# Projection and attention of a transformer layer put into one stage, block by block

## What is computed

```
h    = layernorm(x) * (1 + ca) + sa               # ca, sa from a small product of c
qkv  = h @ qkv_w.T ;  q, k, v per head
raw  = q . k                                      # per head, T x T
score = alpha * tanh(raw / beta) + lam * (soft . soft) / 2 + hexc . Mh . hexc / 6
        # soft = tanh(h @ hex_w.T), hexc = tanh(h @ q6_w.T): 6 columns each
attn = softmax(causal(score)) ;  out = attn @ v
x    = x + ga * (out @ out_w.T) ;  x = x + gb * experts(layernorm(x) * (1 + cb) + sb)
```

## Time and profile before

| | us |
|---|---|
| median of 3 runs | 2112.16 (2109.01 to 2115.98) |
| the profiled execution | 2128.09 |
| its span, first to last instruction | 2126.2 |
| of it, modulation | 0 to 44.2 |
| projection | 44.2 to 242.9 |
| first loads of attention, to the first exp | 242.9 to 275.7 |
| attention, first exp to last exp | 275.7 to 1322.7 |
| output and router | 1322.7 to 1584.9 |
| experts | 1584.9 to 2126.2 |

### The profile page before, as it was taken

One profiled execution on the slowest core, in us unless ns is written; L12 is line 12 of the kernel. 1 busy time (PEld: TensorE's weight loads), 2 busy tenths in 40 slices (PEclk: granted clock), 3 DMA queues, 4 the chain that ended last, 5 costly groups with the idle time before them and its releaser, 6 DMA issues. The chain is left out here.

```text
span 2126.2 us, 37447 instructions
## 1 busy us (share of the span) xinstructions
PE 1851.9 (87%) x10466; PEld 1181.5 (56%) x10467; DVE 1217.2 (57%) x2548; ACT 1282.3 (60%) x1387; POOL 350.3 (16%) x375
## 2 busy tenths in 40 slices
PE   2978189999899999989989998859819999999997
PEld 1433044444444444444444443748719999999997
DVE  5544167777677777777767777667422332332332
ACT  4332089899798998989979998124303223223222
POOL 1321200000100001000000000322441222222222
PEclk7988699999999999999989999879959999999999
DMA  3455690703306033160430600761146666666663
GB/s 125 141 174 180 169 187 12 142 5 79 78 11 142 5 81 76 24 128 5 90 67 11 141 6 11 227 203 39 64 156 187 191 173 182 187 175 179 190 175 84
DMA packets 157468, 239.44 MB, mean 113 GB/s; under 512 B 17808, under 2 KB 91408, under 8 KB 157264
## 3 DMA queue, kind: packets, MB, share of 16 engines
q1 hardware_dynamic: 143664, 219.57, 38.6%
q0 software_dynamic: 13440, 17.97, 4.4%
q10 hardware_dynamic: 288, 1.08, 0.1%
HBM read 173.53 MB, written 65.03 MB: 112 GB/s over the span
## 5 line engine op out<-in xcount | busy, mean ns | idle before, releaser
L772 DVE SCALAR_TENSOR_TENSOR probs<-probs,scal,bil_ps 128x512 f32<-128x512 f32 (+1 forms) x1152 | 773.9, 715 | 279.2 <-ACT probs L735 183.2
L735 ACT ACTIVATE probs<-raw_ps 128x2048 f32<-128x2048 f32 (+1 forms) x288 | 519.4, 1803 | 85.6 <-PE raw_ps L670 85.6
L742 ACT ACTIVATE probs<-probs 128x2048 f32<-128x2048 f32 (+1 forms) x288 | 530.3, 1841 | 33.9 <-DVE probs L772 33.8
L682 PE MATMUL bil_ps<-u_mv,w_st 128*128 128x512 f32 (+3 forms) x1280 | 469.2, 425 | 54.5 <-DVE probs L772 31.3
L682 PEld LDWEIGHTS bil_ps<-u_mv,w_st 128*128 128x128 f32 x1280 | 216.0, 191 | 412.7 <-DVE probs L772 377.9
L1439 ACT ACTIVATE hid_t<-fc_ps,b 128x128 f32<-128x128 f32 x576 | 156.3, 383 | 406.4 <-PE fc_ps L1406 254.8
L670 PE MATMUL raw_ps<-q_mv,k_st 128*128 128x512 f32 (+3 forms) x1280 | 332.4, 386 | 55.0 <-DMA v_sb<-v_rows 47.3
L697 PE MATMUL o_ps<-probs,v_sb 128*32 128x512 f32 (+3 forms) x2560 | 301.1, 552 | 0.5 <-POOL probs L655 0.5
L670 PEld LDWEIGHTS raw_ps<-q_mv,k_st 128*128 128x128 f32 x1280 | 209.2, 191 | 145.6 <-ACT probs L735 69.7
L1406 PE MATMUL fc_ps<-rows_t,w 128*128 128x128 f32 x2304 | 271.2, 276 | 0.0
L1406 PEld LDWEIGHTS fc_ps<-rows_t,w 128*128 128x128 f32 x2304 | 265.3, 193 | 0.1
(11 more groups left out here) (182 smaller groups left out, 1185.4 us busy)
## 6 DMA issues: line engine op xcount, KB each, us to landing
w<-in_w SPq DMA_DIRECT2D x80, 1024.0 KB, 11.9
q_mv<-q_split SPq DMA_DIRECT2D x128, 128.0 KB
rows<-x_rows SPq DMA_DIRECT2D x72, 130.0 KB, 2.0
v_rows<-v_st SPq DMA_DIRECT2D x8, 1024.0 KB, 5.2
k_st<-k_split SPq DMA_DIRECT2D x64, 128.0 KB
k_st<-k_split SPq DMA_DIRECT2D x128, 64.0 KB
v_sb<-v_rows SPq DMA_DIRECT2D x32, 256.0 KB
o_t<-o_sb SPq DMA_DIRECT2D x32, 256.0 KB, 2.2
```

Of the source, the lines that this page charges most:

```text
L682: mm = pe.matmul(bil_ps[:, hd % 2, column:column + width], w_st[:, kt * P:(kt + 1) * P], u_mv[:, hd, qb * BLK + query:qb * BLK + query + w ...
L735: act.activation(probs[:, s % NBUF, :, first:BLK], raw_ps[:, :, first:BLK], ACT.Tanh).then_inc(tanh_ready, 1)
L742: act.activation(scores, scores, ACT.Exp).then_inc(exp_ready, 1)
L772: dve.scalar_tensor_tensor(scores, scores, scal[:, ALPHA:ALPHA + 1], bil_ps[:, hd % 2, first:BLK], ALU.mult, ALU.add).then_inc(sum_ready, 1)
```

## The change

Projection and attention become one stage, `stage_front`. The new order is over 8 blocks of 512 positions (batch 0 first), and in each over the 4 groups of heads: 32 iterations of 3, 7, 11 or 15 steps, 288 steps as before, written out and not looped.

- Blocks 0 and 1 are projected at the start of the stage (HEAD_PARTS), in five banks. The parts of blocks 2 to 7 are cut in 19 pieces each (T0 and T1 turn the rows round, then C, Q0, L, Q1, Q2, V0, Q3, V1, G; all but T and L in halves) and go into steps of the attention, at most one in a step, 114 of them and the guard of block 1; the last is at step 206. They share one bank, `part_ps`. `keep_clock`, which could multiply something in steps without a piece, has no step (FILL_AT is empty).
- Within a step on PE: raw of s+3, bias of head 2, values, bias of head 3, bias of head 0 of the next step, the piece, bias of head 1.
- The work on the results moves. DVE copies a part out of its bank (`empty`) between the second and the third sum of a step; in attention the split in high and low goes to POOL, which also normalises the rows (blocks 0 and 1: DVE), between its masks. ACT keeps the tanh of the codes.
- The 32 normalising steps on ACT at the end of modulation go; x is loaded a second time, block by block.
- k, q and the bias operands hold heads in pairs on rows 0 to 63 and 64 to 127 without zeros; a raw or bias product runs over 64 or 50 rows. There are two buffers; SP loads keys, bias operands and values of iteration n when iteration n-2 has been read. Keys and values of all blocks up to the current one are loaded again in each iteration.

```diff
-STEPS = [step for qb in range(NBLK) for step in
-         [(qb, [(kt, 0, 0, BLK)]) for kt in range(TPB * qb)] + diagonal_steps(qb)]
+BLOCKS = [(i // NBLK, i % NBLK) for i in range(N_BLK)]
+ITERS = [(i, g) for i in range(N_BLK) for g in range(NG)]
+STEPS = [(it, pieces) for it, (i, _) in enumerate(ITERS) for pieces in block_steps(BLOCKS[i][1])]
...
+KEYS_AT = {max(LAST[it - 2] - PE_LEAD, 0): it for it in range(2, len(ITERS))}
+BIAS_AT = {LAST[it - 2] - PE_LEAD + 1: it for it in range(2, len(ITERS))}
+VALUES_AT = {LAST[it - 2] + 1: it for it in range(2, len(ITERS))}
...
-            act.wait_ge(shift_ready, 1)
-            for n in range(NTILE):
-                tile = x_sb[:, n * D:(n + 1) * D]
-                act.activation(tile, tile, ACT.Identity, bias=shift[:, n:n + 1], scale=rstd[:, n:n + 1])
...
+            for o in ("Q0", "C", "Q1", "Q2", "L", "Q3"):
+                store(0, o)
+            load_keys(0)
+            store(0, "V1")
+            sp.wait_ge(pad_ready, 1)
+            load_codes(0)
+            store(0, "G")
+            load_bias(0)
+            load_values(0)
+            load_rows(2)
+            load_keys(1)
+            load_bias(1)
+            load_values(1)
+            for o in ("Q0", "C", "Q1", "Q2", "L", "Q3", "V1"):
+                store(1, o)
+            load_rows(3)
+            for s in range(NSTEP):
...
-                        mm = pe.matmul(raw_ps[:, hd, column:column + width],
-                                       k_st[:, hd // 2, kt * P:(kt + 1) * P],
...
+                        row = hd % 2 * ROWS
+                        mm = pe.matmul(raw_ps[:, hd, column:column + width],
+                                       k_st[row:row + ROWS, p, hd // 2, kt * P:(kt + 1) * P],
...
+                if s + PE_LEAD - 1 < NSTEP:
+                    bilinear(s + PE_LEAD - 1, (2,))
+                weighted_values(s)
+                if s + PE_LEAD - 1 < NSTEP:
+                    bilinear(s + PE_LEAD - 1, (3,))
+                if s + PE_LEAD < NSTEP:
+                    bilinear(s + PE_LEAD, (0,))
+                for i, o, half in SLOT.get(s, []):
+                    project(i, o, half)
...
+                if s + PE_LEAD < NSTEP:
+                    bilinear(s + PE_LEAD, (1,))
```

More of the change, by code:

```diff
@@ L360, in stage_projection @@
[L360 to L418, removed]
-                    (st_w, N_W), (st_s, N_S), (st_l, N_L), (st_g, N_G), (st_v, N_V)]:
-                sp.wait_ge(s, ST_0 + 16 * n * B * NBLK)
@@ L612, in store_out, with bank_of @@
-        def store_out(sp, it, qb):
-            sp.wait_ge(o_ready, it * NBLK + (O_0 + qb + 1))
-            sp.dma_start(dram["o_t"][ds(it * P, P), qb * BLK:(qb + 1) * BLK],
-                         o_sb[:, qb % 2, :]).then_inc(o_stored[qb % 2], 16)
+        N_QK, N_W, N_S, N_L, N_G, N_V = 2, 4, 4, 4, 2, 1
+        N_KEYS, N_BIAS, N_CODES = 10, 6, 2
+        N_EARLY = 5
+        early_banks = [part_ps[:, :]] + [raw_ps[:, hd, :] for hd in range(HG)]
+        def bank_of(part):
+            n = PART_NUMBER[part]
+            return early_banks[n % N_EARLY] if n < len(HEAD_PARTS) else part_ps[:, :]
@@ L642, in _ @@
+            store_out(len(ITERS) - 1)
+            for s in o_stored:
+                sp.wait_ge(s, 16 * len(ITERS) // 2)
         @block.gpsimd
         def _(pool):
[L645 to L657 removed]
+            done = [0]
@@ new lines, in keep_clock, with raw_scores @@
+            def keep_clock(part):
+                i, o = part
+                if o == "C":
+                    pe.wait_ge(code_ready, i + 1)
+                else:
+                    pe.wait_ge(emptied, EMPTIED[i, o])
+                pe.matmul(part_ps[:, :], ident[:, :], modrow[:, 0:BLK], start=True, stop=True)
+            def raw_scores(s):
+                it, pieces = STEPS[s]
+                p = it % 2
+                if s == FIRST[it]:
+                    pe.wait_ge(keys_in[p], 16 * N_KEYS * (it // 2 + 1))
+                if s:
+                    pe.wait_ge(tanh_ready, s)
@@ L739, in exp @@
                 first = first_column(s)
-                act.wait_ge(sum_ready, it * (HG * NSTEP) + (HG * (s + 1) + SUM_0))
+                act.wait_ge(sum_ready, HG * (s + 1))
                 scores = probs[:, s % NBUF, :, first:BLK]
                 act.activation(scores, scores, ACT.Exp).then_inc(exp_ready, 1)
-            tanh(0, 0)
-            def iteration(it, last):
-                for s in range(NSTEP):
-                    if s + 1 < NSTEP:
-                        tanh(it, s + 1)
-                    elif not last:
-                        tanh(it + 1, 0)
-                    exp(it, s)
@@ L754, in _ @@
-            with act.Fori(0, NIT - 1) as it:
-                iteration(it, False)
-            iteration(NIT - 1, True)
+            for i in range(EARLY):
+                make_codes(i)
+                for m in range(4):
+                    high_half(i, m)
+            tanh(0)
+            for s in range(NSTEP):
+                if s + 1 < NSTEP:
+                    tanh(s + 1)
+                exp(s)
+                for i, o in DONE_AT.get(s - 2, []):
+                    if o == "C":
+                        make_codes(i)
@@ new lines, in _ @@
+            for t in range(TPB):
+                normalise(dve, then_wait, 0, t)
+            dve.memset(w_st[:, :, :].bitcast(F32), 1.0).then_inc(pad_ready, 1)
+            dve.memset(v_st[:, :, :, HD:VW], 1.0).then_inc(ones_ready, 1)
+            for n, (i, o) in enumerate(HEAD_PARTS):
+                if o != "C":
+                    empty(i, o)
+                if i == 0 and o[0] == "Q":
+                    normalise(dve, then_wait, 1, int(o[1]))
+            for s in range(DVE_LEAD):
+                for hd in range(HG):
+                    score_sum(s, hd)
```

790 lines of the change are left out of this document (486 added, 304 removed).

## The result

The changed kernel takes 2060.32 us (median of 4, 2056.47 to 2067.46), the kernel before 2112.49 in the same runs: a ratio of 0.9757 (95% interval 0.9724 to 0.979), 52 us less. The forecast was 2041, range 1960 to 2100. The profiled execution took 2067.46 us, its span 2065.7.

What follows compares the result with a forecast made beforehand. The prediction took ACT to bound attention (busy 978.5 of 1047 us), but not the projection. Terms -169 + 47 + 23 + 55 + 3.5 + 6 + 10 - 47 = -71.5, on 2112.2, gave 2041 us, range 1960 to 2100.

Steps and rivals of the forecast that it cites:

- Term 1: Front, up to ACT's first exp: it comes at 107 us and not at 275.7, a gain of 169 us.
- Term 2: First iterations: ACT waits for loads queued on SP behind block 1's stores; 47 us lost, seventh exp at 156.
- Term 3: Start of batch 1, short iterations from 16: SP's loads and stores take longer than the steps; 23 us lost.
- Term 4: Attention steps with a piece: PE's summed work, 4.15 us, exceeds ACT's 3.56; 55 us lost.
- Term 5: Smaller losses: tanh of codes on ACT 3.5 us, POOL's splits 6, PE at clock 0.50 after long waits 10.
- third rival: PE's clock falls in attention, in steps without a piece and waits: 5.4 us a step, 2189 at 80 steps; chance 0.12.
- Term 6: ACT's old 70 us of waits in attention go, except 0.75 us at 31 changes of query block: 47 saved.
- first rival: Pieces cost nothing in attention, as raw products on different rows run side by side: 1988 us; chance 0.20.

Runs made afterwards that it cites:

- the order run: Changed kernel with SP storing block 1 behind the keys and bias operands of iteration 2, not ahead of them: 2058.85 us.
- fill_all: Changed kernel with a filler, one f32 product of 512 columns that nobody reads, in each of the 173 steps without a piece: 2008.69 us.
- raw_128: Changed kernel with raw products over all 128 rows again, bias products left at 50 rows: 2327.71 us.
- rows_128: Changed kernel with raw and bias products both over both heads of a pair, 128 and 114 rows, no filler: 2069.92 us.

## Why the prediction was right, and where it was not

The direction, the range and, at the full clock, the bound were right. The sum of ACT's waits in attention was forecast at 164 us (terms 2 to 5 without the tanh of 3.5, and 23 left of term 6), and 170 came. But that was luck, as its parts were not right: the 55 us of the pieces did not come, and the clock and the changes of iteration cost some 40 and up to 30 us more than taken.

- **Term 1, the front: right.** Forecast 169 us and the first exp at 107; 170 and 105.30. Its chain held too: Q0 was stored from 63.86 us (forecast 63) and the first keys loaded from 85.53 (86.4).
- **Term 2, first iterations: right in size.** Forecast 47; ACT's waits add up to 33.6 us up to the 13th exp and about 6 more up to the 20th. The seventh exp came at 150.01 (forecast 156), behind the keys of iteration 2 as said. The cause was put too narrowly: the order run shows that the queue's order does not matter; that the transfers fill the DMA engines is the likely reason.
- **Term 3, start of batch 1: right.** Forecast 23; waits in steps 144 to 167 add up to 25, the longest 4.93 us at 716.21 and 6.34 at 755.19. No run took it apart.
- **Term 4, the pieces: wrong.** Forecast 55, measured nothing. The step that failed is the sum of PE's work, 3.1 us plus 1.05. The piece itself was sized well (1.06 from its start to the next product, 1012.56 to 1013.62), but the rest was too large, since raw and bias products overlap: with a filler PE needs 3.57 us and not 4.15. And the sum took a place in the queue to be all one. Without a piece PE waits in each step for DVE to empty a bank of `bil_ps`, and the piece stands in just that wait. The same product costs 0.68 us where the wait is used up already, and 0.7 to 1.1 us a step where it stands elsewhere. "The shortest step that PE can do" was the wrong quantity; the ring of bias products and sums was the right one, as the runs that moved one product in it show.
- **Term 5, the clock: far too small.** Forecast 10 us for a dozen waits; the filler gives back 52. The third rival had the mechanism (PE with less to do since raw runs side by side) and nearly the price (5.4 us a step, though its own terms add up to 5.57; measured 5.07). Its place was too narrow: of the 295 us at 0.50 in attention some 130 lie in steps with a piece, much the same share as in the others. It had too many steps for its number: its 80 at 1.85 us would be 148 us.
- **Term 6: too good.** All of the old waits went, but a change of iteration costs ACT 0.86 and 0.92 us, 1.8 in all, and not 0.75:

```profile
937.42 1.92 ACT L895 ACTIVATE probs<-probs 128x2048 f32<-128x2048 f32 x1 [0.86 <-DVE probs L962]
...
944.74 1.91 ACT L895 ACTIVATE probs<-probs 128x2048 f32<-128x2048 f32 x1 [0.92 <-DVE probs L962]
```

 In 31 changes that is up to 30 us more than taken. Why a change costs this is not shown. What POOL's splits cost, forecast at 6 us in term 5, no run took apart.
- **Not in the sum**: the step itself, 3.62 us and not 3.56, some 12 us in the 192 full steps off the diagonal; ACT's busy time, 994 us where the forecast has 982, shows as much. That is the larger part of what parts 2041 from 2060. Its cause is not shown; in fill_all, too, the step is no shorter with the clock held, so the ring may set it.

The first rival had the signature that it named (raw under 0.9 us, no gap of ACT in steps with a piece) and gave 1988; with the clock held, the kernel comes to 2008.7. What was said against it, that raw's four weight loads take 0.77 us one after the other, fell too: at 962.96 the four take 0.40. Its rule of the Trainium skill, TensorEngine Tiling (Array Packing), "Theoretical Speedup", up to twice the rate for 64 rows, is borne out in part: 1.20 us became 0.83 to 0.96, not 0.60. The rule against it in the Trainium skill, TensorEngine Tiling (Array Packing), "Key Properties", a drain at a change of tiling, agrees with raw_128 against rows_128: with changes of rows around raw the way from head 1's bias product to the values is 0.4 us longer (1.99 and 1.59). That its cost would show for the pieces did not come true; the piece with its changes fits into the ring's wait.

What stays open: which event starts each fall of the clock. Some follow a wait for loads, as in the kernel before; the one at 983 us follows the narrow steps of an iteration's end.

## What to carry to other kernels

Work that is merged into another stage should be weighed against the waits of the engine that takes it, at the place in its queue where it will stand, and not against the sum of its work: here one and the same product was free in one place, and cost 0.7 and 1.1 us a step in two others. When a change makes an engine's work shorter, look at what that work kept up; the paired products were faster and let the clock fall, and a useless product in the idle steps was worth 52 us. Wrong terms of opposite sign give a right time, so forecast what each term would show in the trace, and read that first.

## What was not expected of the hardware

- Less work made the kernel slower: 60 products cut from 512 to 8 columns cost some 24 us, and 173 products of 512 columns that nobody reads gained 52; the granted clock over attention was 0.80 and 0.96 in these runs, and 0.87 in the change alone.
- The lower clock stayed for 55 us (985 to 1040) while PE was busy 46 of them.
- Products on rows 0 to 63 and 64 to 127 overlapped, four in 0.83 us where four on 128 rows took 1.20; raw on 128 rows between bias products on 50 made the step some 0.4 us longer than with both on the rows of a whole pair.
